# Writing the state's change into a lent PSUM bank by halves, padding thin products, and a new order of tasks

## The reference

```
x1 = x + attn_a(layernorm(x))          # token mixing and a per-channel scan over time
x2 = x1 + ffn(layernorm(x1))           # 8 experts, 128 -> 512 -> 128: (silu(z Wg) * (z Wu)) Wd, softmax weights
x3 = x2 + attn_b(layernorm(x2))        # 16 heads, each with an 8 x 8 state
x4 = x3 + ffn(layernorm(x3))           # the same experts again
```

```
tmp = einsum('bhj,bhjk->bhk', a * knt, wkv)
wkv = d[..., None] * wkv - knt[..., None] * tmp[:, :, None, :] + vt[..., None] * rk[:, :, None, :]
out = einsum('bhij,bhj->bhi', wkv, rt)
```

## Time and profile before

| what | us |
|---|---|
| median of 3 runs | 919.16 (919.03 to 919.55) |
| the profiled execution, its own time | 917.1 |
| span of its instructions | 915.4 |
| PE busy | 871.5 |
| PE weight loads busy | 738.6 |
| DVE busy | 558.2 |
| POOL busy | 405.9 |
| ACT busy | 396.8 |

### The profile page before, as it was taken

The page is one execution under the profiler, slowest core; times in us unless marked ns, Lnnn a source line. Parts: engine busy times, 40 slices in busy tenths (PEclk is TensorE's granted clock), DMA queues, the critical chain, the costliest instruction groups (busy, mean ns, idle before and its releaser), DMA issues.

```text
span 915.4 us, 14063 instructions
## 1 busy us (share of the span) xinstructions
PE 871.5 (95%) x5282; PEld 738.6 (81%) x5282; DVE 558.2 (61%) x935; ACT 396.8 (43%) x873; POOL 405.9 (44%) x287
## 2 busy tenths in 40 slices
PE   7999999989998999999999999997999889999997
PEld 5987887878777989998676788986998768788886
DVE  5687542688739983219698796896214849543332
ACT  6262346533572333335637435333333343544332
POOL 3553220088306865636354663785654513211111
PEclk9999999999999999999998899999999979999999
DMA  9400000011001100022110111110002211000000
GB/s 285 100 1 1 1 1 1 1 69 47 24 1 47 58 13 24 1 89 76 66 47 24 47 47 47 48 47 12 24 1 93 93 47 58 1 1 12 1 1 13
DMA packets 20712, 35.90 MB, mean 39 GB/s; under 512 B 3062, under 2 KB 9636, under 8 KB 20644
## 3 DMA queue, kind: packets, MB, share of 16 engines
q1 hardware_dynamic: 20644, 35.00, 11.6%
HBM read 21.36 MB, written 13.63 MB: 38 GB/s over the span
## 4 chain that ended last, share of the span: by engine, by line
PE 81%; DVE 13%; issue 3%; ACT 1%; POOL 1%; SPq 0%; DMA 0%; DVEq 0%; POOLq 0%; ACTq 0%
PE bank L1274 79%; DVE sh_buf L1796 2%; PE bank L1300 1%; DVE w_a L2019 1%; DVE states L2017 1%; DVE state L1920 1%; DVE backs L2000 1%; DVE state L1931 1%; DVE normed L1664 0%; POOL rstd L905 0%; ACT sh_buf L1097 0%; DVE low L1702 0%; DVE work L1914 0%; DVE stats L1647 0%; DMA w_a<-in_Wo 0%
## 5 line engine op out<-in xcount | busy, mean ns | idle before, releaser
L1796 DVE TENSOR_TENSOR sh_buf<-sh_buf,bank 128x512 f32<-128x512 f32 x256 | 172.9, 684 | 266.8 <-PE bank L1274 214.1
L1274 PEld LDWEIGHTS bank<-w_down,sh_buf 128*128 128x128 f32 x2048 | 275.4, 195 | 54.4 <-DVE sh_buf L1796 30.5
L1274 PE MATMUL bank<-w_down,sh_buf 128*128 128x128 f32 x2048 | 296.3, 283 | 20.1 <-DVE sh_buf L1796 19.6
L1097 ACT ACTIVATE sh_buf<-bank 128x512 f32<-128x512 f32 x256 | 152.5, 599 | 275.9 <-PE bank L1274 216.7
L1274 PE MATMUL bank<-z_hi,w_lo 128*128 128x512 f32 x512 | 231.1, 451 | 0.8 <-ACT z_hi L1077 0.8
L1274 PE MATMUL bank<-z_lo,w_hi 128*128 128x512 f32 x512 | 204.4, 399 | 0.0
L1274 PE MATMUL bank<-z_hi,w_hi 128*128 128x512 f32 x512 | 204.3, 399 | 0.0
L981 POOL TENSOR_TENSOR x<-x,y_weighted 128x512 f32<-128x512 f32 x63 | 86.8, 1377 | 226.4 <-ACT y_weighted L1211 214.1
L1274 PEld LDWEIGHTS bank<-z_lo,w_hi 128*128 128x128 f32 x512 | 97.6, 191 | 24.2 <-DVE z_lo L1807 1.4
L1274 PEld LDWEIGHTS bank<-z_hi,w_lo 128*128 128x128 f32 x512 | 99.2, 194 | 13.3 <-issue 3.7
L1274 PEld LDWEIGHTS bank<-z_hi,w_hi 128*128 128x128 f32 x512 | 99.0, 193 | 9.0
(11 more groups left out here) (225 smaller groups left out, 960.0 us busy)
## 6 DMA issues: line engine op xcount, KB each, us to landing
trans_spill<-state SPq DMA_DIRECT2D x16, 512.0 KB, 2.6
backs<-trans_spill SPq DMA_DIRECT2D x16, 512.0 KB, 3.3
backs<-keep_spill SPq DMA_DIRECT2D x4, 1024.0 KB, 5.6
x<-in_x SPq DMA_DIRECT2D x4, 256.0 KB, 5.5
backs<-in_w_gate SPq DMA_DIRECT2D x4, 256.0 KB, 5.3
backs<-in_w_up SPq DMA_DIRECT2D x4, 256.0 KB, 5.6
keep_spill<-rkv SPq DMA_DIRECT2D x4, 256.0 KB, 2.5
keep_spill<-low SPq DMA_DIRECT2D x4, 256.0 KB, 2.6
```

The lines of the kernel that those rows point to most:

```text
L1097: act.activation(s_buf[:, m % 2, :], bank_of("gate", m)[:], ACT.Silu).then_inc(S["silu_done"], 1)
L1274: return pe.matmul(dst, lhs, rhs, start=start, stop=stop, **kw)
L1796: dve.tensor_tensor(h_buf[:, m % 4, :], s_buf[:, m % 2, :], bank_of("up", m)[:], ALU.mult).then_inc(S["h_done"], 1)
```

## The change

1. **Steps.** The removed part is no longer made in `prod_w`. The planner lends DVE a PSUM bank (`lend_w`, key `("change", t)`) for each removal step, 128 x 512, half a state. DVE then works by halves of 512: removed part into the bank, bank = outer - bank, `locst` half += bank; the same for the second half. Six operations of 512 take the place of three of 1024. W3 now holds the first two, W4 the third and fourth, W5 the last two. W3 waits for POOL's `outer`, which only W5 did.
2. **Sums.** `PE_SUMS` is chosen anew: 13 of 14 T2 and 13 of 14 W2 are on PE, before 11 and 12. Three 1024-element reductions leave DVE, three sums of 8 products come to PE.
3. **Adds.** `ADDS` names 21 experts (before: the last one) whose output is scaled and added by DVE in four operations; the bank `y` is then held until that is done. ACT's and POOL's tasks for 20 experts go.
4. **Thin products padded.** Products with 3, 25, 26 or 64 rows or columns of weights (`tokB`, `front_hidden` 5, `back_out`) take 128 rows, with zeros or repeats in the tiles; the number of streamed columns stays.
5. **Start.** `wo` gets 14 warm-up products, DVE makes the first `in_z` copy after ACT's other one, and POOL's weight splits from the third on wait for the second `inner` (`kvr_used`) and not for the second receptance product (`kvr_full`).
6. **Order.** All task times, weights and offsets are new, the planner has another account of PE's clock (`slowed`), and `finish` is two tasks. So the order on each engine and the banks are new everywhere.

```diff
-PE_SUMS = dict(T2=[0, 1, 1, 0, 1, 1, 0, 1, 1, 1, 1, 1, 1, 1, 1, 0], W2=[0, 1, 1, 1, 1, 0, 1, 1, 1, 1, 1, 1, 1, 1, 1, 0])
+PE_SUMS = dict(T2=[1, 1, 1, 1, 1, 1, 0, 1, 0, 1, 1, 1, 1, 1, 1, 1], W2=[0, 0, 1, 1, 1, 1, 1, 1, 1, 1, 1, 1, 1, 1, 1, 1])
+ADDS = [1, 0, 0, 0, 0, 0, 0, 1, 1, 0, 0, 0, 0, 0, 0, 0, 0, 0, 0, 0, 1, 0, 0, 0, 0, 1, 0, 0, 0, 1, 0, 0, 0, 0, 0, 0, 0, 0, 1, 1, 1, 0, 0, 1, 0, 0, 1, 1, 0, 0, 0, 1, 1, 1, 0, 1, 0, 1, 1, 1, 0, 1, 0, 1]
...
+            out += [pe(("lend_w", t), 0.0, on("dve", "W1", t), *((summed,) if on_pe else ()), takes=((("change", t), on("dve", "W5", t)),)),
+                    dve(("W3", t), HALF_STEP, summed, on("pe", "lend_w", t), on("pool", "outer", t), port=not on_pe),
+                    dve(("W4", t), HALF_STEP, on("dve", "W3", t), on("pool", "readout", t - 1), port=not on_pe)]
...
                     elif i >= 2:
-                        pool.wait_ge(S["kvr_full"], 2)
+                        pool.wait_ge(S["kvr_used"], 2)
...
-                keep_busy(bank_named[name], 8)
+                keep_busy(bank_named[name], 14)
...
-                    free[name] = (S["y_scaled"], e + 1)
+                    free[name] = (S["x_added"], e + 1) if ADDS[e] else (S["y_scaled"], weighed(e) + 1)
...
+            def lend_w(t):
+
+                name = BANK["change", t]
+                lent_w[t] = free.get(name)
+                free[name] = (S["step_upd"], t + 1)
...
-                mm(dst[:, 0:2 * C], ones3[:], b_row[:], start=False)
-                mm(dst[:, 2 * C:3 * C], hid[0:LOW, 5, tok], b_low[0:LOW, 2, :]).then_inc(S["tokB_full"], 1)
+                mm(dst[:, 0:2 * C], ones_r[:], b_row[:], start=False)
+                mm(dst[:, 2 * C:3 * C], hid[:, 5, tok], b_low[:, 2, :]).then_inc(S["tokB_full"], 1)
...
-                    dve.tensor_tensor(prod_w.rearrange("p (h i k) -> p h i k", h=H, i=N),
-                                      kh[:, i, :].rearrange("p (h i) -> p h i", h=H).unsqueeze(3).broadcast_to((P, H, N, N)),
-                                      summed.unsqueeze(2).broadcast_to((P, H, N, N)), ALU.mult).then_inc(S["sum_w_used"], 1)
+                    if lent_w[t]:
+                        dve.wait_ge(*lent_w[t])
+                    removed_part(t, 0)
+                    step.wait()
+                    dve.wait_ge(S["outer_rdy"], t + 1)
+                    change_part(t, 0)
                 else:
-                    dve.wait_ge(S["sum_w_used"], removals(t))
                     dve.wait_ge(S["readout_rdy"], t)
-                    step.inc(dve.tensor_tensor(locst, locst, prod_w, ALU.subtract))
+                    step.wait()
+                    step.inc(add_part(t, 0))
+                    step.wait()
+                    removed_part(t, 1)
...
+            def change_part(t, half):
+                step.inc(dve.tensor_tensor(change(t), half_of(outer, half), change(t), ALU.subtract))
+
+            def add_part(t, half):
+                return dve.tensor_tensor(half_of(locst, half), half_of(locst, half), change(t), ALU.add)
...
+                    dve.wait_ge(S["sum_w_used"], removals(t))
+                    change_part(t, 1)
                     step.wait()
-                    dve.tensor_tensor(locst, locst, outer, ALU.add).then_inc(S["step_upd"], 1)
+                    add_part(t, 1).then_inc(S["step_upd"], 1)
```

More of the change, by code:

```diff
@@ L116, in on, with added @@
     return engine, key
+def added(e):
+    return on("dve" if ADDS[e] else "pool", "add", e)
 def experts():
@@ L147, in experts @@
         after = (on("pe", "down", g - 1, 1),) if g else ()
-        out.append(pe(("down", g, 0), 0.41, on("dve", "hidden", g), *after, takes=((("y", e), on("act", "weigh", e, 1) if e < PASSES * E - 1 else on("dve", "add_last")),) if f == 0 else ()))
+        out.append(pe(("down", g, 0), 0.41, on("dve", "hidden", g), *after, takes=((("y", e), on("dve", "add", e) if ADDS[e] else on("act", "weigh", e, 1)),) if f == 0 else ()))
         out.append(pe(("down", g, 1), 0.41, on("pe", "down", g, 0)))
[L150 to L157, removed]
+    for e in range(PASSES * E):
+        before = ((added(e - 1),) if e else ()) + ((on("dve", "combine", e // E),) if e % E == 0 else ())
+        if ADDS[e]:
+            out.append(dve(("add", e), 1.1, on("pe", "down", FC * e + FC - 1, 1), on("dve", "combine", e // E), *before))
+        else:
+            out += [act(("weigh", e, 0), 0.63, on("pe", "down", FC * e + FC - 1, 1), on("dve", "combine", e // E), *before),
+                    act(("weigh", e, 1), 0.63, on("act", "weigh", e, 0)),
+                    pool(("add", e), 1.26, on("act", "weigh", e, 1), port=True)]
     return out
@@ L529, in commit @@
                 time += SWITCH
-            self.busy = [(a, b) for a, b in self.busy if b > begin - GATE]
-            if begin > WARM and sum(min(b, begin) - max(a, begin - GATE) for a, b in self.busy) < GATE / 2:
-                time *= 1.75
-                self.cold += time * 3 / 7
-            self.busy.append((begin, begin + time))
+            more = time * slowed(self.busy, begin)
+            time += more
+            self.cold += more
+            self.busy = self.busy[-24:] + [(begin, begin + time, WORK.get(o.key[0], 500))]
         free = self.banks() if o.takes else ()
@@ L556, in schedule @@
         ops += ffn_input(q)
-    ops += [pe(("biases",), 0.7, on("pe", "gate", 24), takes=((("biases",), on("dve", "biases")),)), dve(("biases",), 2.5, on("pe", "biases")),
-            dve(("restart", 0), 1.6, on("dve", "mix", 3))]
-    ops += [sp(("store", j), 4.0, on("pool", "add", E * (BLOCKS + j + 1) - 1) if j < BLOCKS - 1 else on("dve", "add_last")) for j in range(BLOCKS)]
+    ops += [pe(("biases",), 0.7, on("pe", "gate", 24), takes=((("biases",), on("dve", "biases")),)), dve(("biases",), 4.4, on("pe", "biases")),
+            dve(("restart", 0), 1.75, on("dve", "mix", 3))]
+    ops += [sp(("store", j), 4.0, added(E * (BLOCKS + j + 1) - 1)) for j in range(BLOCKS)]
     plan = Plan(ops)
```

231 lines of the change are left out of this document (145 added, 86 removed).

## The result

The changed kernel takes 882.95 us in the median (882.86 to 885.59) against 919.36 beside it, a ratio of 0.961 with an interval of 0.959 to 0.963: 36 us faster. The forecast was 910.7 with a range of 899 to 923. The direction was right, the size was four times too small.

A forecast was written before the change was run, and what follows sets the result against it. PE was taken as the bound, busy 871.5 of 915.4 us. Terms +3.1 (sums), -2.0 (start), -9.6 (order) and zeros gave -8.5: from 917.1 to 908.6, or 910.7 for the median, range 899 to 923.

The forecast's parts named there:

- Padding, term 0: Thin products on PE: the same number of columns is streamed whatever the rows hold, so 0 us for the products.
- Order, term -9.6: New order on all engines: a little under a fifth of 53.5 us of PE's idle time and clock cost goes.
- the three sums: T2 and W2 sums moved to PE: +5.6 us of PE issue, 2.5 given back for DVE's reductions, +3.1 on the path.
- Step operations, term 0: Removal steps on DVE: six halves near 684 ns; DVE's work falls by 5.7 us or grows by 6.0, path zero.
- All six: Removal steps on DVE: by the skill's rule, all six new half operations are free of POOL, saving the whole 5.7 us.
- Loads of the engines: Busy times expected after the change: DVE near 568 us, ACT near 374, POOL near 375; 16 records at 26 sums.
- Start, term -2.0: Start of the kernel: more warm-ups and later weight splits save 2.0 us, bounds -2.5 and +1.5.
- Adds, term 0: Twenty more experts' adds on DVE: DVE +22.4 us, covered by its idle time, so 0 on the path.
- The lent bank: Rival, removal steps: PE waits for PSUM banks, one more 1.4 us wait in each of 14 steps, 930 us; chance 0.12.
- The adds were not late: Rival on DVE: six adds delay a `hidden` that PE needs and W3 waits on `outer`, 926 us; chance 0.06.
- The order does what it could: Rival: three fifths of idle time at `hidden` (11.6) and half the clock's 21 (10.5) go, 898 us; chance 0.17.
- The sign of being wrong: PE's waits at `hidden` staying at 19 us with the clock still 0.86 around `front` and `back`, or PE waiting for banks.

The follow-up runs named there:

- E8: The changed kernel with the task offsets, weights and nearness that the planner of before had: 912.6 us.
- E3: The changed kernel with three step operations of 1024 back in place of the halves, in its own order, lent bank unused: 916.48 us.
- E7: The changed kernel with three step operations of 1024, the planner told so and making its order anew with offsets not searched for it: 894.45 us.
- E4: The changed kernel with the 20 adds that went to DVE given back to ACT and POOL: 886.1 us.
- E1: The kernel before with the thin products padded to 128 rows and nothing else: 908.53 us, ratio 0.988.
- E2: The changed kernel with the thin products unpadded as before, its own order kept: 898.64 us.
- E15: The changed kernel planned with the account of PE's clock that the planner of before had, all offsets as new: 883.8 us.
- E10: The kernel before with only the start's two edits, 14 warm-up products and the weight splits waiting for the second `inner`: ratio 0.9995.

## Why the prediction was wrong, by its steps

- **Padding, term 0: the step that failed.** "PE streams the same number of columns" is true, and the products got no shorter. But PE waits at each of 80 changes of row count: `tokB` takes 1.35 us from token to token, of which 0.58 goes when the row counts are made equal. The pairs of `back_out` at 490 us, 0.83 us apart, stand in the same stretch as the sum of the earlier trace rows; I read durations there and in the forms by line, not distances. 11 to 16 us against 0. With 15.2 for it the forecast would have been 895.5, still 12.5 above the result, so the next term failed too.
- **Order, term -9.6, mis-sized; with the steps it gave some 24.** Sum of the change 36.4, less 15.2 for the padding, is 21.2; the three sums were put at +3.1 (not tried by themselves), so order, steps, adds and start made about -24. Of that, adds 3, start 0 to 1. The rest, 20 to 21 us, can't be split between the halves and the order: halves in an order not made for them gave nothing beyond the padding (E8), and the searched order without them costs 33.5 (E3). Only the 11.5 of E7 for the halves, with an order planned but not searched without them, stands beside it.
- **Step operations, term 0.** The mechanism was right: halves at 0.686 to 0.696 (forecast 0.684), never over 0.70 with an operand in PSUM. "All six" was not: where DVE makes the sum, the removed part reads two SBUF tiles, in one step of 14 (0.98 and 1.53 us). And I counted only the excess that the trace of before showed, 11.7 us. That planner had kept those operations apart from POOL's, and the cost of keeping apart stood in no row. That this constraint is what was saved fits E7, but no run measures it by itself.
- **Loads of the engines.** DVE 564.9 (forecast 568), ACT 376.1 (374), POOL 370.3 (375), 416 records of sums on PE, that is 26: right.
- **Start, term -2.0.** 1.3 in the trace of the changed kernel, nothing measurable alone.
- **Adds, term 0.** 3, of unknown cause (E4).
- **The rivals.** The lent bank did not starve PE: of the 14 waits that this rival priced, one is there, 1.5 us of a gate product at 510 us, put down to a removed part that frees `sum_w`, as the rival said (it "is held two operations longer"). The adds were not late. "The order does what it could" (898) had the right side and fell short by 15 us. That this equals the padding is partly luck: it had the idle time at `hidden` fall by 11.6 and the clock's cost by 10.5, and they fell by 6.9 and 19.4.
- **The clock.** The sign of being wrong, 480 to 530 us still at 0.86, did not come: that window has 0.97. PE's waits at `hidden` fell from 19.3 to 12.4 us, the longest from 3.4 to 2.1.

**What stays open.** Why the stretches at 1.2 GHz went is not settled. It was not the padding: E1 has the clock of before and E2, in three executions of four, nearly that of the changed kernel. It was not the new account of the clock either (E15). Both the searched order and the freedom of the halves bear on it: E8, without the first, has 0.982 to 0.985, and E3 and E7, without the second, 0.982 to 0.993. Seven of the ten stretches that the kernel before has while PE works begin within 1.3 us of the end of a wait of PE of 1.8 to 3.4 us; the others, at 494, 512 and 808 us, have no such wait ahead of them. The changed kernel has four such waits after its start and two such stretches, at 474 and 515 us, each at the end of a wait of 2.0; ahead of the second PE was busy for 2.59 of 5 us. So fewer long waits explain a part, and no run here shows what became of the three without one.

No version tried beats the changed kernel; E15 equals it.

## What to carry to other kernels

Look for matmuls with few rows or few columns of weights (64 or fewer here) among full ones, and read the distance from start to start around them; group the thin products or pad them, both help, and the padding costs nothing in streamed columns. When a planner or an order keeps two engines apart, the trace shows little of that conflict: price the constraint, not the collisions that are left. And an edit in a kernel with a fixed order can't be judged in the old order or in an unsearched one: here the same operations took 883 and 913 us.

## What the runs showed of the hardware that was not expected

- A change between matmuls of 128 rows and of 3, 26 or 64 rows costs 0.18 to 0.19 us of PE at the full clock, whichever way it goes. Products of 26 rows in a row follow each other after 0.11 us a record, like those of 128, and a change between 97 and 128 rows costs nothing.
- A DVE operation of 512 with two SBUF inputs took 0.68 us alone and up to 2.88 beside POOL; with one of them in PSUM 0.68 to 0.70 in all 82 cases, 73 of them beside POOL.
- Where the clock falls is not fixed: in E10's trace a stretch at 1.2 GHz appears at 184 us and those at 296 and 334 us of the kernel before are gone, with no edit near them, and executions of one kernel differ (E2: 0.988 to 0.997). Effects of a single microsecond can be hidden by this.
